# Attention kernel on one Trainium2 core: half of a probability tile's sum goes into the next tile one step earlier, and the text's end follows the third score

## What is computed

```python
q = rms_norm(linear(x, q_w, q_b), norm_q_w)            # 4 batches x 512 queries, 16 heads of 32
k, v = ...text part of the context...                  # 1344 keys
k_img, v_img = ...image part of the context...         # 257 keys
def attention(q, k, v):
    scores = einsum('bqhd,bkhd->bhqk', q, k) / sqrt(32)
    return einsum('bhqk,bkhd->bqhd', softmax(scores), v)
x = x + tanh(g_xattn) * (linear(attention(q, k, v) + attention(q, k_img, v_img), o_w, o_b))
```

## Time and profile before

| | |
|---|---|
| median of 3 runs | 1761.29 us (1760.61 to 1761.71) |
| the profiled execution's own time | 1759.23 us |
| its span | 1757.9 us |
| mean granted TensorE clock, share of full | 0.995 |
| PE busy | 1692.5 us, 96% |
| DVE busy | 1212.7 us, 69% |
| POOL busy | 876.6 us, 50% |
| ACT busy | 821.1 us, 47% |

### The profile page before, as it was taken

The page is one execution under the profiler, slowest core; times in us unless marked ns, Lnnn a source line. Parts: engine busy times, 40 slices in busy tenths (PEclk is TensorE's granted clock), DMA queues, the critical chain, the costliest instruction groups (busy, mean ns, idle before and its releaser), DMA issues. The chain is left out here.

```text
span 1757.9 us, 24703 instructions
## 1 busy us (share of the span) xinstructions
PE 1692.5 (96%) x8694; PEld 1111.2 (63%) x8694; DVE 1212.7 (69%) x2246; ACT 821.1 (47%) x1519; POOL 876.6 (50%) x316
## 2 busy tenths in 40 slices
PE   5999999999999999999999999997999999999999
PEld 4888878885444445444444444444777778878777
DVE  5776677667888887888878888875545454443565
ACT  4443322336666664666556666661321355554221
POOL 3121312116766664777736667710514466766542
PEclk9999999999999999999999999998999999999999
DMA  9456858646455552555445544221312488876433
GB/s 314 138 178 187 248 174 205 184 162 194 129 149 149 143 135 53 139 147 148 127 121 147 125 113 129 78 83 41 126 43 102 141 276 260 272 261 227 154 116 96
DMA packets 198603, 273.04 MB, mean 155 GB/s; under 512 B 30968, under 2 KB 128008, under 8 KB 197964
## 3 DMA queue, kind: packets, MB, share of 16 engines
q1 hardware_dynamic: 193360, 254.67, 49.2%
q0 software_dynamic: 5120, 16.78, 2.8%
HBM read 198.15 MB, written 106.18 MB: 173 GB/s over the span
## 5 line engine op out<-in xcount | busy, mean ns | idle before, releaser
L1128 ACT ACTIVATE P<-ps 128x512 f32<-128x512 f32 (+1 forms) x832 | 444.1, 596 | 261.4 <-PE ps L989 213.7
L639 DVE TENSOR_REDUCE mp<-ps 128x1 f32<-128x448 f32 x768 | 430.0, 615 | 87.1 <-PE ps L446 86.7
L446 PE MATMUL ps<-Kst,Qst 96*128 96x448 f32 (+1 forms) x1024 | 383.3, 389 | 5.8 <-DVE mp L639 5.5
L1342 POOL TENSOR_TENSOR sacc<-sacc,P 128x2048 f32<-128x2048 f32 x90 | 379.8, 4220 | 12.9
L989 PE MATMUL ps<-Qst,Kst 100*128 100x512 f32 (+1 forms) x832 | 322.2, 408 | 9.1 <-ACT P L1128 8.8
L446 PEld LDWEIGHTS ps<-Kst,Qst 96*128 96x128 f32 x1024 | 192.4, 188 | 213.5 <-DVE mp L639 142.2
L944 PE MATMUL ps<-P,Vg 128*32 128x512 f32 (+2 forms) x1664 | 216.0, 603 | 0.4 <-ACT P L1128 0.3
L815 POOL TENSOR_TENSOR cl<-craw,ch 128x1024 fp32r<-128x1024 f32 (+2 forms) x26 | 62.0, 2386 | 285.6 <-ACT ch L551 285.6
L989 PEld LDWEIGHTS ps<-Qst,Kst 100*128 100x128 f32 (+1 forms) x832 | 152.0, 185 | 69.0 <-ACT P L1128 43.2
L49 PE MATMUL ps<-W,ch 128*128 128x512 f32 (+1 forms) x408 | 162.5, 398 | 0.0
L51 PE MATMUL ps<-W,cl 128*128 128x512 f32 (+1 forms) x408 | 159.7, 391 | 0.0
(11 more groups left out here) (241 smaller groups left out, 3087.7 us busy)
## 6 DMA issues: line engine op xcount, KB each, us to landing
gur<-in_w_gate_up SPq DMA_DIRECT2D x23, 1024.0 KB
Kst<-KHd SPq DMA_DIRECT2D x56, 320.0 KB, 4.8
Vd<-vf SPq DMA_DIRECT2D x50, 256.0 KB, 2.3
craw<-in_ctxT SPq DMA_DIRECT2D x24, 512.0 KB, 4.5
KHd<-sth SPq DMA_DIRECT2D x24, 512.0 KB, 3.5
KLd<-stl SPq DMA_DIRECT2D x24, 512.0 KB, 4.7
dnr<-in_w_down SPq DMA_DIRECT2D x23, 512.0 KB, 3.9
xg<-Xg SPq DMA_DIRECT2D x23, 512.0 KB, 7.9
```

The lines of the kernel that those rows point to most:

```text
L446: pe.matmul(ps[:, bank, 0:c1 - c0], Qst[G % 3][0:96, j, 128 * qt:128 * qt + 128], Kst[G % 2][0:96, j, c0:c1], start=True, stop=True).then_ ...
L639: dve.reduce_max(out, ps[:, bank, 0:c1 - c0], AX.X).then_inc(d_ra, 1)
L1128: act.activation(P[slot(G, kt)][:m, j, :], ps[:m, 2 + (e - 1) % 3, :], ACT.Exp, scale=SCALE).then_inc(a_exp, 1)
L1342: pool.tensor_tensor(sacc[:, h], (P[slot(G, 0)] if kt == 1 else sacc)[:, h], P[slot(G, kt)][:, h], ALU.add).then_inc(g_sum, 1)
```

## The change

```diff
@@ pe_attend, a step's order
-            if kt == 11:
-                text_end(G)
             if kt == 12:
                 both_halves_of_10(G)
...
             place(2)
             scored(2)
+            if kt == 11:
+                text_end(G)
             place(3)
             scored(3)
@@ act_attend
-                    if kt == 11 and j == 1:
+                    if kt == 11 and j == 2:
                         txt_weighed(G)
@@ dve_attend
         def add_half_of_7(G):
-            dve.wait_ge(a_exp, exp_no(G, 7, 3))
-            dve.wait_ge(g_sum, sum_no(G, 6))
-            dve.tensor_tensor(sacc[:, 2:4], sacc[:, 2:4], P[slot(G, 7)][:, 2:4], ALU.add).then_inc(d_add, 1)
+
+            dve.wait_ge(a_exp, exp_no(G, 8, 3))
+            dve.wait_ge(p_pv, pv_no(G, 8))
+            to = P[slot(G, 8)]
+            dve.tensor_tensor(to[:, 2:4], to[:, 2:4], P[slot(G, 7)][:, 2:4], ALU.add).then_inc(d_add, 1)
...
+            elif kt == 10:
+                units(G + 1, at, upto[2] - at)
+                add_half_of_7(G)
+                units(G + 1, upto[2], sum(plan[2:]))
             elif kt == 11:
                 units(G + 1, at, sum(plan))
                 if more:
                     dve_text_maxima(G + 1, ra)
-                add_half_of_7(G)
                 add_to_sum(G, 8, slice(0, 4))
```

## The result

The changed kernel takes 1803.33 us in the median of four runs (1795.7 to 1817.47), the kernel before 1760.99. The ratio is 1.025, with a 95% interval of 1.0207 to 1.0293. It is 42 us slower, on the forecast side, and 6 us outside the range that I had given. I had said 1787.

What follows compares the result with a forecast made beforehand. PE was taken to bound the attention. Twelve groups at +2.25 us (+2.7 held add, -0.45 text's end), less 0.1 and 0.9 for the others, gave +26.0; on the 1761.29 median that is 1787 us, range 1765 to 1797.

Steps and rivals of the forecast that it cites:

- What bounds the kernel: In the attention windows PE sets the time, busy 98.8 of 100 us; a change gains only by removing PE's stalls.
- the 0.08 us of slack at the fourth unit: Step 10, fourth unit behind tile 8's weigh: it needs DVE's reduction of the first unit, with 0.08 us to spare.
- POOL holds the moved add: Step 10: POOL's running half add of tile 7 delays DVE's add, so PE's fourth unit comes 2.68 us later; +2.7 taken.
- mean near 2.8: Sign of being right: the moved add, DVE's line 1222, averages near 2.8 us instead of 1.215.
- The sum without the clock, +26: Whole kernel: twelve groups give +27.0 us, groups 5 and 9 together -0.1, groups 0 and 15 -0.9; sum +26.0.
- Group 0 is not held: Group 0: weigh ends at 436.44, before POOL's half starts at 437.35, so DVE is first; net -0.45 us.
- The text's end gives 0.45 a group: Text's end behind the third score: the next step's held score finds its exponential ready, -0.45 us for PE.
- the rest of DVE's order costs nothing: Group's end: waits for the total over `sacc` and for tile 8's add cost nothing, within 0.1 us either way.
- +2.25: Net per group in twelve groups: +2.7 us for the held add less 0.45 at the text's end.
- The copy on ACT as new wait: Rival at tile 10's halves: the text result's copy ends too late, 0.45 us is lost 16 times, 1794 us; chance 0.10.
- The clock falls: Rival: PE's 2.5 us idle per group drops the clock to 1.2 GHz, twelve falls cost 20 us, 1807; chance 0.08.

Runs made afterwards that it cites:

- The run with one input: Changed kernel with DVE's half add in step 10 replaced by a row maximum of about the same length reading one SBUF tensor: 1762.11 us, ratio 1.0009.
- the filled version: Changed kernel with ten extra, unneeded PE matmuls in step 10 between the third and fourth unit, groups 0 to 14 without 5 and 9: 1783.85 us, ratio 1.0124.
- the run with the half add alone: Changed kernel with the text's end and its copy back in their old places, so only DVE's half add moved: 1817.08 us, ratio 1.0326.

## Why the prediction was wrong

By its own steps:

- *What bounds the kernel, and the 0.08 us of slack at the fourth unit.* Right. All of the loss starts there.
- *POOL holds the moved add.* Right, and by size: the add ended 1.09 us behind POOL's end (1.08 predicted), the fourth unit came 2.60 late (2.68), PE's idle was 2.44 (2.5). The run with one input, at 1220 ns, and the one with POOL behind DVE both remove it. The trace agrees with the rule of the Trainium skill that I had named ("SBUF — State Buffer", Who interferes with whom), except that the add ends 1.08 to 1.09 us behind POOL's end and not its whole 1.22. My "mean near 2.8" for line 1222 was a slip: twelve of 3.0 and three of 1.2 make 2.64, and 2.65 was measured.
- *The sum without the clock, +26.* Right within its own range: 1783.85 with the idle filled is +23. Thirteen groups were held, not twelve, each for a little less than I had.
- *Group 0 is not held.* Wrong. There the add took 2.55 us and PE was idle for 2.05. In this execution the weigh of group 0 ended at 438.15, not 436.44, and POOL had started its half at 437.4 as before. It is one group of fifteen.
- *The text's end gives 0.45 a group, and the rest of DVE's order costs nothing.* Right in direction, too small in size. In the filled version successive groups are 49.45 us apart, by the starts of line 1017, where the kernel before has 47.5: +1.9 net, where I had +2.25. The fourth unit is 2.6 late there, so 0.7 came back and not 0.45. But the gain is only free where PE waits elsewhere. With the half add behind the units, or with the text's end alone, most of it is given back at step 12 by the wait for tile 8's add. I had named that wait and costed it at nothing.
- *The copy on ACT as new wait.* It did not happen: the filled version has no wait of PE there.
- *The clock falls: 0.08.* This is the step that failed: a term of some 20 us stood in no sum and outside the range, on the ground that an idle of 2.5 us costs nothing. The clock fell behind all 13 stretches of the profiled run, and filling them gave back 19.5 us. My price, 12 x 1.7 = 20 us, agrees with that in part by luck: the 1.7 us of one fall (3.4 at half speed) were met in eight of the 13, the others were two and three times as long, and the profiled run lost 34. The chance was wrong because of how I read the trace. From "behind 2.66 us the next matmul was not slow, behind 3.87 it was" I took it that 2.5 us would be harmless. Three faults lie in it.

First, I passed over a fall in the same trace, 8 us ahead of my row and behind a shorter idle. The first matmul takes 0.57, the next ones 0.63, where 0.40 is usual:

```profile
28.79 0.57 PE L49 MATMUL ps<-Kst,Qst 128*128 128x512 f32 x1 [1.97 <-DVE Qst L625]
29.16 0.63 PE L50 MATMUL ps<-Kst,Qst 128*128 128x512 f32 x1
```

Second, one row is no measure, for the same stretch comes out both ways. My row of 2.66 us at 36.91 has its twin in the run with the half add alone, where the clock fell at once:

```profile
37.20 0.77 PE L49 MATMUL ps<-Kst,Qst 128*128 128x512 f32 x1 [2.65 <-DVE Qst L625]
37.76 0.63 PE L50 MATMUL ps<-Kst,Qst 128*128 128x512 f32 x1
```

Third, the fall need not show at the first matmul. In group 3 it begins 1.3 us after PE's return, so only the rows behind it tell. Behind my row of 2.66 us they too are at full pace, so this fault did not bring about the misreading, but it could have.

The range ended at 1797, since I left the falling clock out of it. With both mechanisms in the sum, and the sizes as measured, the number would have been 1761.3 + 23 + 20 = 1804. That is hindsight, and a single run can lie 14 us from it.

## What to carry to other kernels

Before an add with two SBUF inputs is moved on DVE, look at what POOL is doing at the moment when it becomes ready; here a wait that puts POOL second recovered 37 of 42 us. A stall of PE can cost more than its length when the clock falls with it, so keep new stalls short or give PE something to do; 130 unneeded matmuls made the changed kernel 19.5 us faster. And when a wait is removed, work out which wait ends last next: here it was the add of tile 8, and splitting it was worth 4 us more. A single row that shows full speed behind an idle stretch does not show that the next one is harmless.

## What the runs showed of the hardware

- The granted clock of PE fell to 1.2 GHz behind 13 of 13 idle stretches of 2.1 to 2.4 us in the changed kernel's attention, behind 9 of 14 of 1.8 us, 3 of 14 of 1.3 us, and directly behind none of 0.7 us. The fall began between 0 and 1.8 us after PE's return and lasted 3.4 to 10.2 us. The spread of the changed kernel's runs, 1795.7 to 1817.5, goes with their mean clocks, 0.984 to 0.972.
- It fell behind single stretches elsewhere too, and also with a delay. In the changed kernel's own trace PE idles for 1.80 us in the part behind the attention. The first matmuls keep their pace, and 1.4 us later they lose it:

```profile
1280.13 0.47 PE L49 MATMUL ps<-xTh,Kst 128*128 128x512 f32 x1 [1.80 <-DVE xTl L1882]
1280.44 0.39 PE L50 MATMUL ps<-xTl,Kst 128*128 128x512 f32 x1
...
1281.68 0.63 PE L49 MATMUL ps<-xTh,Kst 128*128 128x512 f32 x1
1282.10 0.63 PE L50 MATMUL ps<-xTl,Kst 128*128 128x512 f32 x1
```

  What decides between two stretches of equal length stays open; it was not tried. Nor is the fall in the last group explained, which came with short waits only.
- The moved add ends 1.08 to 1.09 us behind POOL's instruction in every held case: with 1.5 to 1.8 us of POOL left at its start in the changed kernel, and with 0.2 to 0.4 left in the version with the add behind all units. So a hold costs what POOL has left, less 0.14 us of the add's 1.22.
- A held DVE instruction is shown as running: its record covers the wait, 2.94 us for 1.2 us of work. Only the comparison with its free length, or with POOL's timeline, tells a hold from slow work.
